# Side work of the first two query tiles of a sequence, set in another order over TensorE, SyncE and GpSimd

## The reference: what is computed

```python
x = x + attention(layernorm(x))   # 16 heads, latent queries and keys, 64 rotary + 64 plain features, causal softmax
x = x + ffn(layernorm(x))         # shared gated part for every token + 16 experts, top 2 of a softmax router

q = (h @ Wqa @ Wqb)               # per head: 64 plain, 64 rotary features
c_kv, k_pe = split(h @ Wkva)      # 64 latent features shared by all heads, 64 rotary features
scores = softmax(causal(q @ k.T * 128 ** -0.5))
out = (scores @ v) @ Wo
```

## Time and profile before

| | us |
|---|---|
| median of 3 runs | 1568.94 |
| lowest, highest | 1566.73, 1570.32 |
| the profiled execution | 1574.91 |
| its span in the trace | 1572.8 |
| PE busy | 1464.4 |
| DVE, POOL, ACT busy | 1218.1, 1016.7, 1008.5 |

### The profile page before, as it was taken

The page is one execution under the profiler, slowest core; times in us unless marked ns, Lnnn a source line. Parts: engine busy times, 40 slices in busy tenths (PEclk is TensorE's granted clock), DMA queues, the critical chain, the costliest instruction groups (busy, mean ns, idle before and its releaser), DMA issues.

```text
span 1572.8 us, 44810 instructions
## 1 busy us (share of the span) xinstructions
PE 1464.4 (93%) x16413; PEld 1083.3 (69%) x16414; DVE 1218.1 (77%) x2657; ACT 1008.5 (64%) x2399; POOL 1016.7 (65%) x1640
## 2 busy tenths in 40 slices
PE   9889999998899999998999999988999999899990
PEld 4557777776667777676677777776777777667870
DVE  6877778887777888886777778877777888666766
ACT  3666666666567666666666676666666666567770
POOL 4477754553778565666877787668876664286660
PEclk9999999999999999999999999999999999999995
DMA  7457933303464321334452334145343211347518
GB/s 216 81 117 162 169 68 72 60 17 75 80 119 82 70 55 29 62 62 85 85 98 54 59 64 70 33 77 110 68 73 65 60 31 30 100 134 253 158 52 323
DMA packets 331076, 144.66 MB, mean 92 GB/s; under 512 B 278546, under 2 KB 321589, under 8 KB 330872
## 3 DMA queue, kind: packets, MB, share of 16 engines
q1 hardware_dynamic: 305296, 104.57, 33.7%
q10 hardware_dynamic: 18664, 20.52, 4.7%
q0 software_dynamic: 6912, 16.83, 3.4%
HBM read 47.04 MB, written 29.53 MB: 49 GB/s over the span
## 4 chain that ended last, share of the span: by engine, by line
PE 69%; DVE 8%; DMA 6%; ACT 5%; issue 3%; POOL 3%; SPq 3%; POOLq 0%; ACTq 0%; DVEq 0%
PE of_ps L782 28%; PE s_ps L782 25%; PE t_ps L979 14%; DMA qT<-work 3%; DVE pT L1838 2%; DVE smax L1811 1%; ACT work L1192 1%; ACT probs L1314 1%; PE of_ps L1104 1%; SPq L515 1%; ACT pT L1189 1%; PE t_ps L1090 1%; DMA work<-y_exp 1%; SPq L536 1%; DMA hT<-hs 1%
## 5 line engine op out<-in xcount | busy, mean ns | idle before, releaser
L1838 DVE TENSOR_TENSOR pT<-t_ps,pT 128x512 f16<-128x512 f32 (+3 forms) x688 | 410.5, 598 | 130.6 <-ACT pT L1189 127.6
L1189 ACT CAST pT<-t_ps 128x512 f16<-128x512 f32 (+3 forms) x688 | 355.0, 516 | 231.9 <-PE t_ps L979 231.0
L782 PE MATMUL s_ps<-kT,qT 128*128 128x512 f16 (+3 forms) x2112 | 473.9, 337 | 3.9 <-DMA qT<-work 3.9
L979 PE MATMUL t_ps<-id,probs 128*128 128x128 f32 x2304 | 379.4, 279 | 14.6 <-DVE pT L1838 8.1
L979 PEld LDWEIGHTS t_ps<-id,probs 128*128 128x128 f32 x2304 | 257.7, 141 | 98.0 <-issue 48.1
L782 PEld LDWEIGHTS of_ps<-ckv,pT 128*128 128x128 f16 x6912 | 241.0, 98 | 41.2 <-DVE o_sb L1667 9.5
L782 PE MATMUL of_ps<-ckv,pT 128*128 128x64 f16 x6912 | 257.8, 193 | 7.2 <-DVE o_sb L1667 6.5
L782 PEld LDWEIGHTS s_ps<-kT,qT 128*128 128x128 f16 x2112 | 203.1, 98 | 72.8 <-DMA qT<-work 4.8
L1314 ACT ACTIVATE probs<-s_ps,nmax 128x640 f32<-128x640 f32 (+3 forms) x256 | 245.7, 960 | 0.1
L782 PE MATMUL of_ps<-weights,xT 128*128 128x128 f16 (+1 forms) x930 | 198.0, 349 | 18.2 <-DVE work L1635 8.8
L1800 DVE TENSOR_REDUCE nmax<-s_ps 128x1 f32<-128x640 f32 (+3 forms) x200 | 192.4, 962 | 18.4 <-PE s_ps L782 18.1
(11 more groups left out here) (247 smaller groups left out, 2395.7 us busy)
## 6 DMA issues: line engine op xcount, KB each, us to landing
wgu_sb<-wgu ACTq DMA_DIRECT2D x8, 704.0 KB, 5.3
work<-lists SPq DMA_DIRECT2D x40, 128.5 KB, 2.3
qT<-lists SPq DMA_DIRECT2D x40, 128.5 KB, 2.2
x<-x SPq DMA_DIRECT2D x32, 128.0 KB, 2.7
dense<-den SPq DMA_DIRECT2D x32, 128.0 KB
weights<-dense ACTq DMA_DIRECT2D x1, 4096.0 KB
qT<-y_exp SPq DMA_DIRECT2D x16, 256.0 KB, 6.7
work<-y_exp SPq DMA_DIRECT2D x16, 256.0 KB, 9.1
```

What stands on the lines that cost most here:

```text
L782: return pe_.matmul(o, a, b, start=start, stop=stop)
L979: last = pe_.transpose(t_ps[:, h, c * P:(c + 1) * P], probs[:, u % 2, g * L + j * P:g * L + (j + 1) * P], id32[:, :])
L1189: return act.copy(o, i)
L1838: dve.tensor_tensor(pT[:, u % 2, 1, h, 0:w], t_ps[:, h, 0:w], pT[:, u % 2, 0, h, 0:w], ALU.subtract).then_inc(s.lo_p, 1)
```

## The change

The change touches the sections i = 0, 1 and 2 of each sequence; nothing is computed otherwise.

1. **Order on PE, ACT and DVE.** `HOME` and `LATER` let a job be done one section later: `q1` of tile t + 2 leaves section i = 0 for place (0, 1) of section i = 1; `down` leaves the end of i = 0 for (0, 2) of i = 1, and the end of i = 1 for (0, 0) of i = 2. In i = 0 `lat` moves from (1, 0) to (0, 3), `pe1` from (0, 3) to (1, 1), `q0` from (1, 1) to (1, 2). In i = 1 `lat` moves to (1, 0), `pe1` to (1, 2), `q0` from (2, 3) to (2, 0), `gate` behind it from (2, 0) to (2, 1), `up` to (2, 2), `out` from (2, 2) to (3, 0). In the first sequence only `q1` of section 0 moves.
2. **DVE.** The product and the sum of the rotary features are two jobs; both stand behind the norm of the half output, and in i = 1 the sum stands at a new place (3, 0.5) behind a `prob_lo`.
3. **Queries in halves.** Tiles with i = 1 of every sequence have their queries turned by `turn_half_queries`; the first scores wait for the first half only.
4. **SP.** In i = 1 `turn_x2(p)` goes ahead of `turn_keys(n)` and `turn_queries(n)` (it was behind them); `store_dense` and the first `turn_output` shift in i = 1 and 2. In i = 0 the order stays, but `turn_queries(n)` now waits for a `q1` of the next section, with `turn_x2` behind it.
5. **POOL.** The scatter of q in i = 0 and 1 is done in the next section: in i = 1 around the first half of `rope`, in i = 2 around `out_lo`.

```diff
-SECOND = {"lat": (0, 3), "pe0": (1, 1), "half_lo": (1, 1), "pe1": (1, 3), "gate": (2, 0), "up": (2, 1), "out": (2, 2), "q0": (2, 3), "q1": (3, 1),
-          "rope_sum": (3, 0), "half": (3, 0), "half_hi": (3, 1), "rope_hi": (3, 2), "rope_lo": (3, 3), "down": (4, 0), "up_hi": (2, 1), "other_hi": (1, 0)}
-FIRST_TILE = {"gate": (0, 0), "up": (0, 1), "pe0": (0, 2), "pe1": (0, 3), "lat": (1, 0), "q0": (1, 1), "q1": (1, 2), "out": (1, 3),
-              "rope_sum": (1, 2), "rope_hi": (1, 3), "half": (1, 3), "half_hi": (2, 0), "rope_lo": (2, 0), "down": (2, 0), "up_hi": (0, 1), "other_hi": (1, 0)}
+TILE_1 = {"lat": (0, 3), "pe0": (1, 1), "half_lo": (1, 1), "pe1": (1, 3), "out": (2, 2), "q0": (2, 3), "q1": (3, 1),
+          "rope_mul": (3, 0), "rope_sum": (3, 0), "half": (3, 0), "half_hi": (3, 1), "rope_hi": (3, 2), "rope_lo": (3, 3), "other_hi": (1, 0)}
+SECOND = {**TILE_1, "lat": (1, 0), "pe0": (1, 1), "pe1": (1, 2), "q0": (2, 0), "gate": (2, 1), "up": (2, 2), "up_hi": (2, 3),
+          "out": (3, 0), "q1": (3, 1), "rope_mul": (3, 0), "rope_sum": (3, 0.5)}
+TILE_0 = {"pe0": (0, 0), "pe1": (0, 1), "lat": (0, 2), "q0": (1, 1), "rope_mul": (1, 2), "rope_sum": (1, 2), "rope_hi": (1, 3),
+          "half": (1, 3), "half_hi": (2, 0), "rope_lo": (2, 0)}
+FIRST_TILE = {**TILE_0, "gate": (0, 0), "up": (0, 1), "up_hi": (0, 1), "pe0": (0, 2), "lat": (0, 3), "other_hi": (1, 0), "pe1": (1, 1), "q0": (1, 2),
+              "out": (1, 3)}
...
+LATER = {(0, "q1"): (0, 1), (0, "down"): (0, 2), (1, "down"): (0, 0)}
...
+def split_queries(t):
+
+    return t < 2 or t % TB == 1
...
+                if has(p) and i == 1:
+                    turn_x2(p)
                 if has(n) and i == 1:
                     turn_keys(n)
                     turn_queries(n)
...
-                if has(p):
+                if has(p) and i != 1:
                     turn_x2(p)
...
-                    turn_queries(n)
-                if has(q) and i is not None and i < 4:
+                    if split_queries(n):
+                        turn_half_queries(n, 0)
+                        turn_half_queries(n, 1)
+                    else:
+                        turn_queries(n)
+                if has(q) and i in (2, 3):
                     store_dense(q)
...
                     act.wait_ge(q_in[(n - 1) % 2], 16 * ((n - 1) // 2 + 1))
+                    if split_queries(n - 1):
+                        act.wait_ge(half_in[(n - 1) % 2], 16 * ((n - 1) // TB + 1))
...
+                behind = i in (1, 2) and has(q - 1)
+                if behind:
+                    take_slots(q - 1)
+                    scatter_rows(q - 1, 0)
                 if has(p) and i != 1:
                     out_lo(p, 1)
+                    if behind:
+                        scatter_rows(q - 1, 1)
                 if has(n):
-                    rope(n)
+                    rope(n, (lambda: scatter_rows(q - 1, 1)) if behind and i == 1 else None)
...
-                if has(q):
+                if has(q) and i not in (0, 1):
                     scatter(q)
```

More of the change, by code:

```diff
@@ L91 @@
 THIRD = {**MIDDLE, "lat": (0, 2), "pe0": (1, 1), "pe1": (1, 3), "q0": (2, 1), "q1": (2, 3)}
-SECOND = {"lat": (0, 3), "pe0": (1, 1), "half_lo": (1, 1), "pe1": (1, 3), "gate": (2, 0), "up": (2, 1), "out": (2, 2), "q0": (2, 3), "q1": (3, 1),
-          "rope_sum": (3, 0), "half": (3, 0), "half_hi": (3, 1), "rope_hi": (3, 2), "rope_lo": (3, 3), "down": (4, 0), "up_hi": (2, 1), "other_hi": (1, 0)}
-FIRST_TILE = {"gate": (0, 0), "up": (0, 1), "pe0": (0, 2), "pe1": (0, 3), "lat": (1, 0), "q0": (1, 1), "q1": (1, 2), "out": (1, 3),
-              "rope_sum": (1, 2), "rope_hi": (1, 3), "half": (1, 3), "half_hi": (2, 0), "rope_lo": (2, 0), "down": (2, 0), "up_hi": (0, 1), "other_hi": (1, 0)}
-START = {**FIRST_TILE, "pe0": (0, 0), "pe1": (0, 1), "lat": (0, 2)}
+TILE_1 = {"lat": (0, 3), "pe0": (1, 1), "half_lo": (1, 1), "pe1": (1, 3), "out": (2, 2), "q0": (2, 3), "q1": (3, 1),
[6 more added lines that the diff above has]
+              "out": (1, 3)}
 SIDE = [FIRST_TILE, SECOND, THIRD, MIDDLE, LONG, LONG, LONG, LONG]
+HOME = {"lat": -2, "pe0": -2, "pe1": -2, "q0": -2, "q1": -2, "rope_mul": -2, "rope_sum": -2, "rope_hi": -2, "rope_lo": -2,
+        "half": 0, "half_hi": 0, "half_lo": 0, "out": 1, "other_hi": 1, "gate": 2, "up": 2, "up_hi": 2, "down": 2}
+LATER = {(0, "q1"): (0, 1), (0, "down"): (0, 2), (1, "down"): (0, 0)}
 OTHER_SCALES = 3
@@ L104, in places_in, with place_of @@
 def places_in(t):
-    return START if t == 0 else SIDE[t % TB]
+    return (TILE_0, TILE_1)[t] if t < 2 else SIDE[t % TB]
+def place_of(name, tile):
+    t = tile + HOME[name]
+    if not has(t):
+        return t, (None, None)
+    if (t % TB, name) in LATER:
+        return t + 1, LATER[t % TB, name]
+    return t, places_in(t)[name]
 def due(name, tile, t, k, sub):
-    if not has(tile):
-        return False
-    return (k, sub) == (None, None) if not has(t) else places_in(t)[name] == (k, sub)
+    return has(tile) and place_of(name, tile) == (t, (k, sub))
+def split_queries(t):
+    return t < 2 or t % TB == 1
 OPENING = [("lat", 0), ("pe0", 0), ("pe1", 0), ("lat", 1), ("pe0", 1), ("pe1", 1), ("q0", 0), ("q0", 1), ("q1", 0), ("q1", 1)]
@@ L123, in side_jobs @@
     for t in range(NT + 2):
-        jobs = [(name, tile) for name, tile in (("lat", t + 2), ("pe0", t + 2), ("pe1", t + 2), ("q0", t + 2), ("q1", t + 2),
-                                                ("gate", t - 2), ("up", t - 2), ("out", t - 1), ("down", t - 2)) if has(tile)]
-        order += sorted(jobs, key=lambda job: places_in(t)[job[0]]) if has(t) else jobs
+        jobs = [(name, tile) for name, tile in (("lat", t + 2), ("pe0", t + 2), ("pe1", t + 2), ("q0", t + 2), ("q1", t + 1), ("q1", t + 2),
+                                                ("gate", t - 2), ("up", t - 2), ("out", t - 1), ("down", t - 3), ("down", t - 2))
+                if has(tile) and place_of(name, tile)[0] == t]
+        order += sorted(jobs, key=lambda job: place_of(*job)) if has(t) else jobs
     return {job: k for k, job in enumerate(order)}
@@ L143, in q_col @@
 def q_col(t, a, head):
-    return ((head // 8 * 2 + a) * 8 + head % 8 if t < 2 else a * H + head) * P
+    return ((head // 8 * 2 + a) * 8 + head % 8 if split_queries(t) else a * H + head) * P
 SEED = 1597463007.0
@@ L414, in build, with flat_of @@
         early_qs = [flat.rearrange("p (g s h d) -> p g s h d", g=2, s=2, h=8) for flat in early_flat]
+        def flat_of(n):
+            return n if n < 2 else 0
         def q_latent(n, a, g):
-            return early_qs[n][:, g, a, :, 0:NOPE] if n < 2 else qs[:, a, 8 * g:8 * g + 8, 0:NOPE]
+            return early_qs[flat_of(n)][:, g, a, :, 0:NOPE] if split_queries(n) else qs[:, a, 8 * g:8 * g + 8, 0:NOPE]
         def q_rope(n, a):
-            return early_qs[n][:, :, a, :, NOPE:HD] if n < 2 else qs[:, a, :, NOPE:HD]
+            return early_qs[flat_of(n)][:, :, a, :, NOPE:HD] if split_queries(n) else qs[:, a, :, NOPE:HD]
         def rope_heads(n):
             heads = pe_of(n)[:, 0:H, :]
-            return heads.rearrange("p (g h) r -> p g h r", g=2) if n < 2 else heads
+            return heads.rearrange("p (g h) r -> p g h r", g=2) if split_queries(n) else heads
         def pe_of(n):
@@ L521, in turn_half_queries @@
                 sp.wait_ge(*released(f"q{g}", n))
-                done = q_in[n] if g else half_in[n]
-                sp.dma_start_transpose(qT[:, n].rearrange("p s n -> p (s n)")[:, g * HALF:(g + 1) * HALF].rearrange("p (k n) -> p k n", n=P),
-                                       early_flat[n][:, g * HALF:(g + 1) * HALF]).then_inc(done, 16)
+                if has(n - 2):
+                    sp.wait_ge(s.s_made, 2 * (unit_of(n - 2, units(n - 2) - 1) + 1))
+                done = q_in[n % 2] if g else half_in[n % 2]
+                sp.dma_start_transpose(qT[:, n % 2].rearrange("p s n -> p (s n)")[:, g * HALF:(g + 1) * HALF].rearrange("p (k n) -> p k n", n=P),
+                                       early_flat[flat_of(n)][:, g * HALF:(g + 1) * HALF]).then_inc(done, 16)
             def turn_keys(n):
@@ L563, in section @@
                     turn_hidden(q)
-                if has(p) and i == 1:
+                if has(p) and i in (1, 2):
                     turn_output(p, 1)
+                    if has(q - 1):
+                        store_dense(q - 1)
                     load_residual(p)
@@ L926, in side @@
                     project(n, "q0", 0, 512)
-                if due("q1", n, t, k, sub):
-                    project(n, "q1", 512, 512)
+                for m in (n - 1, n):
+                    if due("q1", m, t, k, sub):
+                        project(m, "q1", 512, 512)
                 if due("gate", q, t, k, sub):
@@ L934, in side @@
                     out_projection(p)
-                if due("down", q, t, k, sub):
-                    down(q)
+                for m in (q - 1, q):
+                    if due("down", m, t, k, sub):
```

(45 more changed lines are left out.)

## The result

The changed kernel takes 1587.09 us (median of 4 runs, 1584.87 to 1591.85) against 1569.63 for the kernel before (4 runs beside it, 1566.73 to 1570.47): ratio 1.0108, 95% interval 1.0087 to 1.013. It is **slower by 17.5 us**. The profiled execution took 1587.67 us, its span is 1585.6, 12.8 more than the span of before.

What follows compares the result with a forecast made beforehand. PE, with work in 93% of the span, was taken as the bound. Sequences at 0, -0.95, +1.8 and +4.2 us (+5.05) plus +5.1 for half clock gave +10.2: 1568.9 to 1579.1, say 1579; range 1563 to 1587.

Steps and rivals of the forecast that it cites:

- Halves: First scores of tiles 9, 17, 25: half queries land sooner, removing waits of 2.18, 0.79 and 0.89 us.
- The walk to `out` of tile 16: From gate of tile 14, third sequence: new job order has 8.8 us of gaps, so `out` starts 0.9 us later.
- it enters with the same state: Second sequence: same walk as the third, entered 330.7 us earlier, reaching q1 327.9 earlier; it comes out at -0.95 us.
- x2 ahead of the queries: SP, sections i = 1: query turn issued 16.2 us behind `out` (bounds 14.9 and 17.5), 0.9 us more than before.
- Who is late next: Section 18: ACT waits for tile 19's queries, landing 1.8 us later; PE idles 5 us instead of 0.68 at q1.
- The clock: Behind the 5 us stop at q1 in three sequences: half clock adds 1.7 us each, +5.1 us.
- (1): Rival, section 18: as forecast, but PE keeps its full clock; +5 us, 1574; chance 0.14.
- (2): Rival, job order: ACT and DVE queues add little, `out` starts up to 4.4 us earlier; 1561; chance 0.13.
- (3): Rival, SP order: costs nothing as POOL ends the norm 2 us sooner, walk 0.6 us too long; 1569; chance 0.17.
- (4): Rival, section 18: waits only move, no stop builds up, the 3.3 us gain stays; 1557; chance 0.04.
- The first sequence: Sections 0 and 1 win some 2 us, x2 and its norm take them back: 0, bounds -2 and +1; stop about 3.4.

Runs made afterwards that it cites:

- halves alone: Kernel before with only the queries of tiles with i = 1 turned in halves: 1574.76 us, ratio 0.998 to the kernel before.
- x2 behind: Changed kernel, but in sections i = 1 SP issues the x2 turn behind the keys and queries again: 1581.47 us, ratio 1.0023 to the kernel before.
- x2 first alone: Kernel before with only the x2 turn issued ahead of keys and queries in sections i = 1: 1593.45 us, ratio 1.01 to the kernel before.
- q0 and q1 later: Changed kernel with q0 and q1 behind gate and up in sections i = 2, x2 still first: 1569.14 us, ratio 0.9949 to the kernel before.

## Why the prediction was right in direction and short in size

The forecast was slower by 10.2 us; the medians say 17.5, the two profiled executions 12.8. I take the difference of the two traces at gate of the sections i = 0 and at q1 of the sections i = 2.

| stretch | forecast | measured |
|---|---|---|
| first sequence, up to the gate of its fourth section | 0 | -0.15 |
| second, up to q1 of tile 12 (from -1.49 to +0.15) | -0.95 | +1.64 |
| third, up to q1 of tile 20 (from +2.17 to +5.11) | +1.8 | +2.94 |
| fourth, up to q1 of tile 28 (from +6.02 to +11.32) | +4.2 | +5.30 |
| behind q1, up to gate of the next section, three times | +5.1 | +2.85, +1.98, +2.14 |
| sections that nothing touches | 0 | -3.9 |

**The forecast in medians.** The last line is no effect of the change. Section 4 took 45.2 us in the profiled execution of the kernel before and 43.8 in that of the changed one, and section 15, which holds the same matmuls, 62.6 against 61.8; both at full clock:

```profile
166.30:211.50 45.20, 43.52 (x527) 33.16 (x525) 34.77 (x78) 29.62 (x75) 32.06 (x51) 1.00 0.98 149
```

```profile
166.20:210.00 43.80, 43.10 (x526) 32.97 (x523) 34.59 (x77) 29.56 (x75) 32.10 (x51) 1.00 0.89 148
```

So the profiled execution of before holds nearly 4 us in places that the change leaves alone, most of the 5 to 6 us by which it lay over its median. The touched stretches add up to +16.7, close to the 17.5 of the medians, and this is the number to hold against the forecast of 10.2. The misses to explain are thus 6.5 us, not the 2.6 that the two spans suggest.

**Halves: right.** The first scores of tiles 9, 17 and 25 have no DMA wait, and done alone they gave 3.2 us.

**The walk to `out` of tile 16: right in the third sequence.** 40.95 us behind gate of tile 14 against 40.39, 0.56 later where 0.9 was forecast. The gap ahead of `down` came out as 1.55 us (1.7), those ahead of lat, gate and up at 0.62, 0.59 and 0.36 (0.7, 0.8 and 0.5). **Wrong in the second:** `out` of tile 7 waited there for the turned output.

```profile
389.04 2.38 PE L818 MATMUL of_ps<-weights,oT 128*128 128x256 f16 x12 [2.54 <-DMA oT<-os_]
```

```profile
721.92 1.25 PE L818 MATMUL of_ps<-weights,oT 128*128 128x256 f16 x10 [1.16 <-DMA oT<-os_]
```

In both sequences DVE norms the output half behind lat, and ACT, POOL and SP follow; SP issues the turn at 384.45 and at 718.72, and it takes 4.6 us to PE's start in the second and 3.2 in the third; why is not known. That costs 1.4 us more, and the stop of 2.54 is followed by 3.4 us at half clock (1.7 us):

```profile
389.00:392.50 3.50, 3.46 (x19) 2.48 (x20) 2.10 (x3) 1.71 (x3) 0.36 (x1) 0.56 0.00 0
```

Together 3.1, of which about half is still there at `out` of tile 8: it starts 42.74 us behind gate, where the copied walk gives 41.3 (40.39 + 0.9). The other 1.1 of the 2.6 us by which the second sequence came out over the forecast lie behind `out`: the query turn was issued 16.65 us behind it, not 16.2, and took 9.08 us, not 8.43. The step that failed is "it enters with the same state": I had one walk and copied it.

**x2 ahead of the queries: the right mechanism, a term too small.** The norm ended 13.98 us behind `out` (13.6 to 13.9 forecast). Two of its steps were drawn out, to 1.15 and 1.23 us from 0.19 or 0.20, which is 2.0 us; the sum had 1.9 left of the 3. The estimate by the Trainium skill (SBUF — State Buffer, "SBUF: two separate sides") was 2.5; the trace agrees with its rule, that the small POOL step waits while DVE runs a rotary instruction with two SBUF inputs. DVE ran them from 751.65 to 752.93 and from 755.52 to 756.74; each POOL step had begun 0.19 and 0.04 us behind DVE's start and ended 0.06 and 0.05 us behind its end, so each lost 0.95 and 1.03 us and not DVE's full 1.28 and 1.22. Then x2, the keys and the gap ahead of the queries took 2.99 us from the norm's end, not 2.65. So the queries were issued 16.97 behind `out` rather than 16.2, half of it from the norm's end and half from SP. Counted from `out`, the query turn was late by 1.71 us against the earlier trace rows, not 0.9 (+0.8), and took 9.10 us to ACT's start instead of 8.43 (+0.7). Less the 0.3 that `out` was early, that is about +1.1, all of the miss of the third sequence. The fourth missed by 1.1 too, of which these two terms hold 0.7 (issued 16.64 behind `out`, 8.70 to ACT's start); the rest is not taken apart.

**Who is late next: right.** PE came to the stop 3.5 us earlier (3.3 forecast), ACT waited 8.13 us ("of 6" forecast), the stop was 7.10 where 5 stood in the text: 0.68 + 3.5 + 2.94.

**The clock: right that it falls, the price too small.** I put 1.7 us on each stop, half of a stretch of 3.4. That is what shorter stops have, in the second to fourth sequence of all these traces, wherever a fall came with a stop (read from the clock records of the traces):

| stop of PE, us (kernel) | half clock, us |
|---|---|
| 2.18, 2.17, 2.35 (before) | 3.4, 3.4, 3.4 |
| 2.30 (halves alone), 2.54 (changed) | 3.4, 3.4 |
| 2.03, 3.20, 4.14, 3.70 (x2 behind) | 3.4 each |
| 2.08, 3.48, 4.05, 5.44 (x2 first alone) | 3.4 each |
| 6.38, 7.10 (changed) | 6.8, 6.8 |
| 6.78 (changed) | 10.2 |

The one stop near 5 us (5.44) had 3.4; the three with more were longer than 6. But length alone doesn't set the stretch. In the first sequence, where PE is idle more often, a stop of 2.00 us at the start of section 2, with one of 1.12 us close behind it, came with 3.4 us at half clock in the changed kernel and with 6.8 in each of the runs x2 behind and q0 and q1 later; one of 2.01 there in the kernel before, with one of 1.05 behind it, came with none. And part of the stretch lies within the stop, where it costs nothing. Behind the stop of 7.10 us 4.0 us of work ran at half clock, which costs 2.0, and gate of the next section was late by another 1.98; in the second sequence, where 5.8 us ran so, it was late by 2.85, in the fourth, with 4.4 us, by 2.14. Together 7.0 instead of 5.1. Stops of 2.14 (halves alone), 2.16 and 2.33 (x2 first alone) and 2.25 (q0 and q1 later) had no fall at all, so between 2.0 and 2.35 us it can go either way, and what decides there isn't settled by these traces, nor what made the stretch behind 6.78 longer than that behind 7.10.

**The rivals.** (1), full clock in section 18, fell: it is at 0.91. (2) fell with `out` 0.56 us later than before, not 4.4 earlier. (3) fell with the norm's end on the forecast. (4), that the waits only move and no stop builds up, fell with the stops of 6.38 to 7.10 us; something close to it is what the run with q0 and q1 later shows: it kept the gain of both sections once nobody stood before the queries. I had written that the rows give no way to that, and within the change they don't: it takes another edit, in the section behind.

**The first sequence** had a stop of 2.21 us at q1 of tile 4 (3.4 forecast) and no fall there; its +1.7 for the range wasn't needed. That the sequence came out at 0 is in part luck: ahead of that stop it has the 3.4 us at half clock named above, which the kernel before hasn't and the sum didn't name.

## What to carry to other kernels

SP issued in its order here, so one transfer of 1.2 us moved ahead of two others, and waiting for a late norm, cost 1.0% of the kernel by itself. Ask of each transfer that a move puts in front what it waits for, and who stands still, on which engine, until the one behind it has landed. Work won upstream of such a wait only made the stop longer here (3.5 us of it), and moving the consumer that waits (two projections, by one unit and more, behind two that don't) gave some 25 us where putting the transfer back gave 13. So look for the waiting consumer's place as well as the transfer's. And where a single stop can reach 5 us, price the clock behind it by stops of that length in a trace of the same kernel, with a range, since like stops differed; and count only the part of the stretch that lies beside work.

## What the runs showed that was not expected

The clock falls within a long stop: from the means of the windows (0.56 over 771.3 to 774.5, 0.53 over 436.9 to 441.6) it was full until about 771.7 and 437.2, 4.3 and 2.4 us behind PE's last work. In all the stops of the table the time at half clock was 3.4, 6.8 or 10.2 us; the stop of 6.38 us came with twice the stretch of the one of 5.44. And the turn of the same 128x4096 float16 elements, with nothing changed in it, took 9.10 us to its consumer in the changed kernel, 8.65 with x2 behind, 9.64 with x2 first alone, 8.41 with q0 and q1 later and 8.43 before, all in the third sequence: a landing was not constant to half a microsecond, for a reason that these runs don't show, and where an engine waits for it, that is part of the range.
